# Window attention: row-maximum scores from 512-column matmuls and keys masked per head

## The reference, cut to what matters

```
normed = _layernorm(win, ln1_g, ln1_b)
qkv = normed @ in_w.T + in_b
q, k, v = heads(q), heads(k), heads(v)                 # 8 heads of 16
scores = jnp.einsum('bhsd,bhtd->bhst', q, k) / jnp.sqrt(jnp.float32(dh))
attn = jax.nn.softmax(scores, axis=-1)                 # needs each row's maximum
o = jnp.einsum('bhst,bhtd->bhsd', attn, v)
```

## Time and profile before

| what | us |
|---|---|
| median of 3 runs | 392.28 (391.3 to 393.44) |
| span of the profiled execution | 389.9 |
| PE busy | 364.9 |
| DVE busy | 294.5 |
| ACT busy | 241.8 |
| POOL busy | 167.4 |
| score matmuls for the maxima, 512, line 611 | 54.6 busy |
| one image in the loop | 44.11 |

### The profile page before, as it was taken

The page is one execution under the profiler, slowest core; times in us unless marked ns, Lnnn a source line. Parts: engine busy times, 40 slices in busy tenths (PEclk is TensorE's granted clock), DMA queues, the critical chain, the costliest instruction groups (busy, mean ns, idle before and its releaser), DMA issues. The chain is left out here.

```text
span 389.9 us, 9822 instructions
## 1 busy us (share of the span) xinstructions
PE 364.9 (94%) x3349; PEld 312.5 (80%) x3349; DVE 294.5 (76%) x863; ACT 241.8 (62%) x438; POOL 167.4 (43%) x176
## 2 busy tenths in 40 slices
PE   3679999999999999999999999999999999999874
PEld 2467888888898888888888888888888888888663
DVE  8387888797688768797688868787688868676452
ACT  1426676764959477774958467674858467663540
POOL 6353154454364434544464434544455434441420
PEclk9999999999999999999999999999999999999796
DMA  4223030303222221303122121403122120300101
GB/s 121 40 77 97 23 100 11 102 0 82 73 63 52 49 58 59 102 0 81 58 77 54 46 62 54 108 0 78 57 74 61 40 67 29 79 6 10 45 1 54
DMA packets 31570, 21.94 MB, mean 56 GB/s; under 512 B 22272, under 2 KB 23360, under 8 KB 31552
## 3 DMA queue, kind: packets, MB, share of 16 engines
q1 hardware_dynamic: 31552, 21.71, 20.4%
HBM read 4.92 MB, written 4.19 MB: 23 GB/s over the span
## 5 line engine op out<-in xcount | busy, mean ns | idle before, releaser
L649 PEld LDWEIGHTS p_attn<-vd,probs 128*64 128x64 f32 x1024 | 52.7, 139 | 22.3 <-issue 15.1
L649 PE MATMUL p_attn<-vd,probs 128*64 128x34 f32 x1024 | 62.1, 244 | 2.8 <-ACT probs L910 2.8
L910 ACT ACTIVATE probs<-p_scoreT 128x512 f32<-128x512 f32 x64 | 38.6, 603 | 38.0 <-PE p_scoreT L634 37.5
L465 POOL TENSOR_TENSOR hid_l<-hid,hid_h 128x512 fp32r<-128x512 f32 x30 | 40.4, 1367 | 47.9 <-ACT hid_h L944 45.8
L611 PE MATMUL p_score<-kd_h,qd_h 128*128 128x128 f32 (+1 forms) x512 | 54.6, 249 | 0.8 <-DVE row_max L1158 0.8
L611 PEld LDWEIGHTS p_score<-kd_h,qd_h 128*128 128x128 f32 (+1 forms) x512 | 50.0, 163 | 5.0 <-DVE row_max L1158 1.3
L470 POOL TENSOR_TENSOR y_l<-y,y_h 128x512 fp32r<-128x512 f32 (+1 forms) x17 | 20.6, 1214 | 71.2 <-ACT y_h L924 71.2
L1158 DVE TENSOR_REDUCE row_max<-p_score 128x8 f32<-128x512 f32 x64 | 44.0, 688 | 6.6 <-PE p_score L611 6.6
L634 PE MATMUL p_scoreT<-qd_h,kd_h 128*128 128x256 f32 x128 | 41.3, 322 | 0.0
L457 POOL TENSOR_SCALAR kd_l<-k_l,head_a 128x512 fp32r<-128x512 f32 x16 | 26.7, 1669 | 33.8 <-DVE k_l L1140 20.0
L449 POOL TENSOR_TENSOR rstd<-rstd,minus_half 128x4 f32<-128x4 f32 (+1 forms) x33 | 35.5, 1075 | 2.8
(11 more groups left out here) (183 smaller groups left out, 881.9 us busy)
## 6 DMA issues: line engine op xcount, KB each, us to landing
x_in<-in_x SPq DMA_DIRECT2D x16, 256.0 KB, 2.8
qd_h<-q_h SPq DMA_DIRECT2D x64, 64.0 KB, 2.0
qd_l<-q_l SPq DMA_DIRECT2D x64, 64.0 KB, 2.0
vd<-v_tok SPq DMA_DIRECT2D x64, 64.0 KB, 2.2
out<-out_sb SPq DMA_DIRECT2D x16, 256.0 KB, 2.0
fc_rows<-in_L_conv_fc_w SPq DMA_DIRECT2D x2, 128.0 KB, 2.6
in_w_rows<-in_L_conv_in_w SPq DMA_DIRECT2D x1, 192.0 KB, 2.7
out_w_rows<-in_L_conv_out_w SPq DMA_DIRECT2D x1, 64.0 KB, 2.5
```

What stands on the lines that cost most here:

```text
L465: pool.tensor_tensor(hid_l[:, t], hid[:, t], hid_h[:, t].bitcast(F32), ALU.subtract).then_inc(hid_low[t], 1)
L649: last = pe.matmul(p_attn[64 * win:64 * win + 64, 2 * VB * j:2 * VB * (j + 1)], probs[:, p % 2, win, j, :], vd[:, h.par, 2 * p + win, :, : ...
L910: act.activation(probs[:, p % 2], p_scoreT[:].rearrange("row (win j q) -> row win j q", win=2, j=QUADS), ACT.Exp, scale=SCORE_SCALE).then_ ...
```

## The change: keys masked per head

A new tensor `km_h` holds, for each of the 8 heads, the high part of the keys of the half with all rows but the head's 16 zero. SP fills it: `spread_k` waits for `k_high` and issues eight copies of 16 rows x 512. It stands between `spread_q` and `spread_v` in SP's queue. `b_score` now takes q_h itself as the weights and 512 columns of km_h (8 heads x 64 keys of one window) as the moving operand: 2 matmuls instead of 8 for 128 tokens. It waits for `q_high` and for the eight km_h copies (`km_dma`). The waits for the spread queries and kd_high move to `b_scoreT`. q_h gets a second slot. Both slots of km_h are zeroed once by POOL.

```diff
-        q_h = sb("q_h", [C, HALF], F32R)
+        q_h = sb("q_h", [C, 2, HALF], F32R)
+        km_h = sb("km_h", [C, 2, HEADS, HALF], F32R)
...
+            def spread_k(h):
+
+                sp.wait_ge(k_high, h.n())
+                if h.follows(2):
+                    sp.wait_ge(score_ready[PAIRS - 1], h.n(2))
+                for head in range(HEADS):
+                    rows = slice(DH * head, DH * head + DH)
+                    sp.dma_start(km_h[rows, h.par, head, :].bitcast(F32), k_h[rows, :].bitcast(F32)
+                                 ).then_inc(km_dma, 16)
...
                 spread_q(loop.half(1))
+                spread_k(loop.half(1))
                 spread_v(loop.half(1))
...
+            pool.memset(km_h[:, 0].bitcast(F32), 0.0).then_inc(km_zero_set[0], 1)
             pool.memset(vd[:], 0.0).then_inc(v_const_set, 1)
...
                 pool.memset(qd_l[:, 1].bitcast(F32), 0.0).then_inc(q_zero_set[1], 1)
+                pool.memset(km_h[:, 1].bitcast(F32), 0.0).then_inc(km_zero_set[1], 1)
...
                 if p == 0:
-                    pe.wait_ge(q_high_dma, h.n(times=16 * QUADS))
-                    pe.wait_ge(kd_high[0], h.n())
-                    pe.wait_ge(kd_high[1], h.n())
+                    pe.wait_ge(q_high, h.n())
+                    pe.wait_ge(km_dma, h.n(times=16 * HEADS))
...
-                for j in range(QUADS):
-
-                    for win, rows in ((1, 2 * KEYS), (0, KEYS)):
-                        last = pe.matmul(p_score[0:rows, 2 * KEYS * j:2 * KEYS * (j + 1)],
-                                         qd_h[:, h.par, j, 2 * KEYS * p:2 * KEYS * p + rows],
-                                         kd_h[:, h.par, 2 * p + win], start=True, stop=True)
+                for win, rows in ((1, 2 * KEYS), (0, KEYS)):
+                    window = 2 * p + win
+                    last = pe.matmul(p_score[0:rows, :], q_h[:, h.par, 2 * KEYS * p:2 * KEYS * p + rows],
+                                     km_h[:, h.par, :, KEYS * window:KEYS * (window + 1)], start=True, stop=True)
...
             def a_q(h):
                 act.wait_ge(q_ready, h.n())
-                if h.follows(1):
-                    act.wait_ge(q_high_dma, h.n(1, times=16 * QUADS))
+                if h.follows(2):
+                    act.wait_ge(q_high_dma, h.n(2, times=16 * QUADS))
+                if h.follows(2):
+                    act.wait_ge(score_ready[PAIRS - 1], h.n(2))
+                if h.follows(2):
+                    act.wait_ge(q_low, h.n(2))
...
             def a_k(h):
...
+                if h.follows(1):
+                    act.wait_ge(km_dma, h.n(1, times=16 * HEADS))
+                if h.follows(1):
+                    act.wait_ge(k_low, h.n(1))
```

More of the change, by code:

```diff
@@ L231, in build @@
         ident_set, const_ready = sem("ident_set"), sem("const_ready")
-        q_zero_set, v_const_set = sems("q_zero_set", 2), sem("v_const_set")
+        q_zero_set, v_const_set, km_zero_set = sems("q_zero_set", 2), sem("v_const_set"), sems("km_zero_set", 2)
         wT_ready, wT_kept, bias_ready, bias_kept = sem("wT_ready"), sem("wT_kept"), sem("bias_ready"), sem("bias_kept")
@@ L242, in build @@
         v_ready, v_kept = sem("v_ready"), sem("v_kept")
-        q_high_dma, q_low_dma, v_dma = sem("q_high_dma"), sem("q_low_dma"), sem("v_dma")
+        q_high_dma, q_low_dma, v_dma, km_dma = sem("q_high_dma"), sem("q_low_dma"), sem("v_dma"), sem("km_dma")
         kd_high, kd_low = sems("kd_high", 2), sems("kd_low", 2)
@@ L352, in spread_q @@
                     head_pair = slice(32 * j, 32 * j + 32)
-                    sp.dma_start(qd_h[head_pair, h.par, j, :].bitcast(F32), q_h[head_pair, :].bitcast(F32)
+                    sp.dma_start(qd_h[head_pair, h.par, j, :].bitcast(F32), q_h[head_pair, h.par, :].bitcast(F32)
                                  ).then_inc(q_high_dma, 16)
@@ L381, in prologue @@
                 spread_q(loop.half(0))
+                sp.wait_ge(km_zero_set[0], 1)
+                spread_k(loop.half(0))
                 sp.wait_ge(v_const_set, 5)
@@ L384, in prologue @@
                 sp.wait_ge(q_zero_set[1], 2)
+                sp.wait_ge(km_zero_set[1], 1)
             def step_even(loop, more, c):
@@ L395, in step_odd @@
                     spread_q(loop.half(2))
+                    spread_k(loop.half(2))
                     spread_v(loop.half(2))
@@ L619, in b_scoreT @@
                 if p == 0:
+                    pe.wait_ge(q_high_dma, h.n(times=16 * QUADS))
                     pe.wait_ge(q_low_dma, h.n(times=16 * QUADS))
+                    pe.wait_ge(kd_high[0], h.n())
+                    pe.wait_ge(kd_high[1], h.n())
                     pe.wait_ge(kd_low[0], h.n())
@@ L876, in a_q @@
                 act.wait_ge(q_ready, h.n())
-                if h.follows(1):
-                    act.wait_ge(q_high_dma, h.n(1, times=16 * QUADS))
-                act.activation(q_h[:], p_a[0][:], ACT.Identity, bias=qkv_b[:, 0:1]).then_inc(q_high, 1)
+                if h.follows(2):
[4 more added lines that the diff above has]
+                    act.wait_ge(q_low, h.n(2))
+                act.activation(q_h[:, h.par], p_a[0][:], ACT.Identity, bias=qkv_b[:, 0:1]).then_inc(q_high, 1)
             def a_k(h):
@@ L1130, in a_q @@
                     dve.wait_ge(q_low_dma, h.n(1, times=16 * QUADS))
-                dve.scalar_tensor_tensor(q_l[:], p_a[0][:], qkv_b[:, 0:1], q_h[:].bitcast(F32),
+                dve.scalar_tensor_tensor(q_l[:], p_a[0][:], qkv_b[:, 0:1], q_h[:, h.par].bitcast(F32),
                                          ALU.add, ALU.subtract).then_inc(q_low, 1)
```

## The result

The changed kernel takes **415.78 us** (median of 4 runs, 414.87 to 416.64), against 392.27 for the kernel before in the same comparison: a ratio of 1.0605, interval 1.0569 to 1.0641. The forecast was 403.5 with a range of 395 to 411. The direction was right, the size only half of what came. The profiled execution has a span of 413.1 us against 389.9, so 23.2 us are to be found.

The account below looks back on a forecast made before the run. PE was taken as the bound, busy 94% of the span. Prologue waits, less 0.46 us in each of six images, plus half 15 and +2.0 for the clock gave +11.2 on 392.28: 403.5 us, range 395 to 411.

Parts of the forecast that it names:

- Copies of k: SP's queue: 0.63 us an issue, last copy landing 11.5 us after the first qd_h copy; PE waits 1.2 in even steps.
- The rivals of cheap issue: Copies on SP: 0.45 us an issue gives 392 us (chance 0.10); issue almost free gives 386 (chance 0.04).
- Their threshold: Cheap copies on SP: the case decides at 0.49 us an issue, from where the even step has no wait.
- Zeroing: POOL's memset of km_h in the prologue: the first rstd of layer norm comes 1.5 us later.
- Score matmuls: PE's score blocks: two 512-column matmuls, 0.47 us; each block gives 0.17 to 0.28, taken as 0.22, or 0.2 for pairs 0 and 1.
- The sum: Whole kernel: delays added half by half, +10.85 after half 2, -0.46 for each of six images, +9.2 at half 15, +11.2 with clock.
- What of the wait is given back: Start of odd halves: the widening against POOL's two hid_l puts PE 0.6 us behind, bounds 0.15 and 1.0.
- the upper bound of 1.0: Start of odd halves: if the widening falls into the second hid_l, PE is 1.0 us behind.
- the 43.2 to 44.1 that the prediction gave as its sign: Loop image: to take 43.65 us or so, within this range, in place of 44.11.
- Clock: PE's clock: the 6.4 us wait in half 0 makes it fall, those of halves 1 and 2 perhaps; estimate +2.0 us.
- The rival that spoke of a falling clock: Loop, around the even boundary: clock falls, 3.2 us each; three times gives 413 us, all seven 425; chance 0.14.
- the +1.15 forecast for them: Half 15: +0.6, minus 0.44 for pairs 2 and 3, +1.0 for a slow qd_l issue; from +8.05 to +9.2.

Follow-up runs that it names:

- The better place: Changed kernel with SP issuing the eight copies of k between those of q's high part and those of q's low part: 396.18 us.
- the four copies: Changed kernel with four 32-row copies for km_h instead of eight of 16 rows, same bytes, the two heads of a pair not separated: 396.82 us.
- the run with a warm clock: Changed kernel with 22 matmuls of 512 columns, result unused, put in PE's list ahead of half 0's scores: 413.87 us.

## Why the prediction was off, point by point

- **Copies of k: right, and it is the cause.** Eight issues in 4.95 us, 2.0 to landing, 1.19 of wait in the odd halves of the loop (1.66 in its first), none in the even ones but its first, which waits 2.26, half 0 at +7.92 (forecast +7.95). Ten waits, as said. The better place and the four copies both take 19 us away. The rivals of cheap issue are refuted. (Their threshold was off: with PE's arrival at 10.3 and landing at 2.0 the even step has no wait below 0.46 us an issue, not 0.49; at a measured 0.62 it changes nothing.)
- **Zeroing: right.** 1.5 forecast; 1.4 between half 0's starts with and without its move.
- **Score matmuls: the size was right where PE is alone, but not what arrives.** The block of pair 2 has a pitch of 0.46 (188.21 to 188.67). By busy time a block gives 0.15 rather than 0.22. The step that failed is in "The sum": pairs 0 and 1 of the even half were booked with 0.4, and pair 2 with 0.22, as bringing SP's copies forward. From the even half's first score block to the first copy it takes 9.35 us (207.44 to 216.79) against 9.42 (189.18 to 198.60): 0.07 arrived of 0.62. The traces show where: pair 1's block still starts 1.66 after pair 0's (before 1.69), since it waits for pair 0's maximum; and the first transposed matmul follows pair 1's block after 0.88 instead of 0.75, since the moved waits stand ahead of it. That is 0.55 us an image. The run with the waits behind the score block adds a third reason: without them the transposed scores follow pair 1's block after 0.57, but SP's first copy still comes only 0.06 sooner, because ACT, which makes `probs`, is not ready. So 0.62 could not have arrived even without the moved waits; the pitch of a block was not its worth there.
- **What of the wait is given back: two errors.** The widening fell into the second hid_l in every odd half of the loop, the upper bound of 1.0, where I took 0.6. The second lay outside all bounds: **the moved waits into b_scoreT stand nowhere in the sum.** I costed the new wait ahead of the score block and the waits on ACT, and passed over three waits that moved to directly behind the widening. They cost 0.39 in an odd half of the loop, where the widening is on the path; moving them away made it 0.36 shorter. Together the transposed scores of an odd half come 1.39 later (1.03 at the score block, 0.36 behind it), where the forecast had 0.6.
- The savings that did not arrive (0.55) and these two errors (0.79) make the image +0.91 instead of -0.46, at 45.01 us outside the 43.2 to 44.1 that the prediction gave as its sign: six images are 8.2 us, two thirds of the 12 missed in the span.
- **Clock: right in kind, too small, and the second part of the miss.** +2.0 was taken for the whole kernel. Half 0 alone lost at least 2.6 (the run with a warm clock) and half 1 came 3.1 later than forecast (+13.3 against 7.75 + 2.5); the clock is also at 0.77 to 0.80 from 92 to 100 us and at 0.50 at 364 to 368. The rival that spoke of a falling clock (413 to 425) met the time, but by luck: in the loop the granted clock fell once, in half 3, for some 0.46 us (45.47 to half 5, then 45.01 an image); from 100 us on it is 1.00 there, and the image is long at full clock.
- The last two halves lost more than the +1.15 forecast for them: half 13 to 15 takes 45.91 against 44.01. The late issue in that place gave a wait of 2.3 us. The rest I leave open.

## What to carry to other kernels

This change moved work from PE to a DMA and paid in issues on the queue, 0.6 us a copy and 4.95 for eight: count what the waiting engine's data stand behind there, and put the copies that are wanted first at the front. A wait that is moved is an edit of its own, even if it is always fulfilled. In a loop, where its threshold is worked out in a register, it cost 0.3 to 0.4 us each time behind the releaser that the path runs through; in the written-out image the same waits in the same order cost nothing (0.06 behind the widening). Put such a wait where the engine still has work queued, as behind the score block here, which took the gap in the odd halves from 0.45 to 0.06. And the gain of shorter matmuls must be followed to the next wait for another engine's answer; here 1.21 us of saved work were 0.76 at most, and only after the copies, the waits and the zeroing had been moved.

## What the runs showed of the hardware that I had not expected

- In the loop, one fulfilled wait more, with a register operation for its threshold, costs PE 0.29 us behind the widening (0.35 against 0.06), three cost 0.39. In half 15, written out with constant thresholds, neither costs anything: 0.06 with the one (345.99 to 346.05) and with the three (350.23 to 350.29, copies of k between those of q). By the records of PE's queue it goes with what runs behind the widening's end: nothing (0.06), two records (0.31), the register operation and two (0.35), or that and three (0.45). No experiment isolates that.
- A copy of 16 rows takes SP as long to issue as one of 32: 4.95 us for eight, 2.45 for four.
- A widening that starts while POOL's subtraction runs ends 0.28 us behind it: 211.61 and 211.89 before, 185.79 and 186.07 after. In the even half it starts 0.17 before the subtraction ends, is done 0.28 behind it (209.25 and 209.53) and loses next to nothing: 0.45 against 0.43 us alone.
- PE at half clock did not come back at once when it had work again: it was at 0.50 from 28 to 40 us though PE was busy 3.95 us of the last four. Work given to PE in one gap (22 matmuls in half 0) moved most of the fall to the next gap in the execution that was traced: 0.86 and 0.72 instead of 0.50 from 28 to 36 us, and 0.50 at 48 to 52.
- Shorter blocks did not bring their result forward as much as their pitch says: in the even half DVE's reduction starts 0.91 us after the block's start (207.44 to 208.35), against 0.94 (189.18 to 190.12), though the next matmul starts 0.17 earlier (0.57 after the block's start against 0.74). Why is open.
